# A transformer layer on one core: the last query tile's products are spread over the first attention step, and the first score maxima move one tile earlier

## The reference

```
x = x + attention(layernorm(x))
x = x + ffn(layernorm(x))

attention(h):   q = h @ Wq              # 32 heads of 32 features
                k, v = h @ Wkv          # one key head and one value head, shared by all
                scores = q k^T / sqrt(32) + slope[head] * (key position - query position)
                scores = -inf above the diagonal
                return (softmax(scores) @ v) @ Wo
ffn(h):         w = (6-bit codes of qweight - zero_point) * scale
                return h @ w^T + bias
```

## Time and profile before

| | us |
|---|---|
| median of 3 runs | 813.38 |
| lowest and highest | 812.87, 813.59 |
| the profiled execution's own time | 815.24 |
| its span | 813.5 |
| PE busy | 802.1 (99% of the span) |
| DVE busy | 596.2 (73%) |
| ACT busy | 370.5 (46%) |
| POOL busy | 427.7 (53%) |

### The profile page before, as it was taken

One profiled execution on the slowest core, in us unless ns is written; L12 is line 12 of the kernel. 1 busy time (PEld: TensorE's weight loads), 2 busy tenths in 40 slices (PEclk: granted clock), 3 DMA queues, 4 the chain that ended last, 5 costly groups with the idle time before them and its releaser, 6 DMA issues.

```text
span 813.5 us, 13624 instructions
## 1 busy us (share of the span) xinstructions
PE 802.1 (99%) x4608; PEld 582.3 (72%) x4608; DVE 596.2 (73%) x1592; ACT 370.5 (46%) x728; POOL 427.7 (53%) x311
## 2 busy tenths in 40 slices
PE   7999999999999999999999999999999999999997
PEld 5788888888656555656565555688887888888886
DVE  5885575657878889988888997364647779684878
ACT  2757355312466777676666665221401141041322
POOL 1000000000389988899898888522746288363465
PEclk9999999999999999999999999999999999999999
DMA  9867666566556555665556645452064523500112
GB/s 344 309 216 250 226 242 231 174 191 195 159 133 147 134 144 144 153 160 134 133 159 168 166 108 178 153 176 90 1 226 146 171 79 111 191 35 1 39 66 104
DMA packets 71389, 125.84 MB, mean 155 GB/s; under 512 B 7460, under 2 KB 16708, under 8 KB 71240
## 3 DMA queue, kind: packets, MB, share of 16 engines
q1 hardware_dynamic: 70592, 123.66, 49.6%
q10 hardware_dynamic: 728, 1.32, 0.5%
HBM read 85.61 MB, written 38.94 MB: 153 GB/s over the span
## 4 chain that ended last, share of the span: by engine, by line
PE 91%; DMA 4%; POOL 2%; DVE 1%; issue 1%; ACT 1%; ACTq 0%; SPq 0%; DVEq 0%; POOLq 0%
PE p_s L869 12%; PE p_st L898 10%; PE p_o L909 10%; PE p_o L808 7%; PE p_s L808 6%; PE p_o L922 5%; PE p_s L977 5%; PE p_s L979 5%; PE p_s L978 5%; PE p_o L810 4%; PE p_s L810 3%; PE p_s L1001 3%; PE p_s L1002 3%; PE p_st L1002 2%; PE p_st L1001 2%; PE p_st L977 2%
## 5 line engine op out<-in xcount | busy, mean ns | idle before, releaser
L1462 DVE CUSTOM_DVE_ANT_0 spill<-p_s,mask 128x128 bf16<-128x128 f32 (+3 forms) x512 | 219.5, 483 | 41.2 <-PE p_s L869 40.9
L1168 ACT ACTIVATE pt<-p_st 128x512 f32<-128x512 f32 (+1 forms) x352 | 178.1, 562 | 101.8 <-PE p_st L898 101.6
L637 POOL TENSOR_SCALAR_AFFINE_SELECT pt<-pt 128x512 f32<-128x512 f32 x128 | 88.0, 700 | 234.7 <-ACT pt L1168 234.7
L869 PE MATMUL p_s<-kst,xt 98*128 98x128 f32 (+3 forms) x512 | 151.3, 343 | 0.9 <-DVE mx L1462 0.7
L898 PE MATMUL p_st<-xt,kst 100*128 100x512 f32 (+1 forms) x352 | 129.7, 388 | 0.3 <-ACT pt L1168 0.2
L869 PEld LDWEIGHTS p_s<-kst,xt 98*128 98x128 f32 x512 | 91.7, 189 | 52.9 <-DVE mx L1462 42.5
L644 POOL TENSOR_TENSOR pt<-pt 128x1536 f32<-128x1536 f32 x32 | 112.3, 3508 | 2.7
L909 PE MATMUL p_o<-pt,vst 128*32 128x512 f32 (+3 forms) x1024 | 83.1, 442 | 0.0
L650 POOL TENSOR_TENSOR pt<-pt 128x1024 f32<-128x1024 f32 x32 | 76.7, 2396 | 0.0
L898 PEld LDWEIGHTS p_st<-xt,kst 100*128 100x128 f32 x352 | 64.7, 191 | 13.6 <-issue 5.6
L808 PE MATMUL p_o<-xt,wqh 128*128 128x512 f32 x136 | 53.1, 400 | 0.8 <-DVE xt L1618 0.8
(11 more groups left out here) (206 smaller groups left out, 1619.4 us busy)
## 6 DMA issues: line engine op xcount, KB each, us to landing
xt<-qh_d SPq DMA_DIRECT2D x64, 256.0 KB
qh_d<-qh SPq DMA_DIRECT2D x32, 256.0 KB, 2.1
ql_d<-ql SPq DMA_DIRECT2D x32, 256.0 KB, 2.2
xt<-ql_d SPq DMA_DIRECT2D x32, 256.0 KB
o_d<-o_st SPq DMA_DIRECT2D x32, 256.0 KB, 2.1
ob<-o_d SPq DMA_DIRECT2D x32, 256.0 KB, 4.6
xs<-in_x_t_dram SPq DMA_DIRECT2D x28, 256.0 KB, 5.4
xin<-in_x_dram SPq DMA_DIRECT2D x14, 512.0 KB, 5.9
```

What stands on the lines that cost most here:

```text
L637: pool.affine_select(out=own, in_=own, compare_op=ALU.is_ge, fill=0.0, base=0, pattern=[[0, 4], [1, P]], channel_multiplier=-1).then_inc(c ...
L869: pe.matmul(scores_of(n), qst[s % 4][0:R_MAX, j, qb * P:(qb + 1) * P], kst[0:R_MAX, b * S:b * S + keys], start=True, stop=True).then_inc(s ...
L1168: act.activation(pt[s % 2][:, j:j + heads, PT_AT[kb]:PT_AT[kb] + KB_LEN[kb]], p_st[:, place(k) % 3, 0:heads * KB_LEN[kb]].rearrange("p (j ...
L1462: dve.tensor_tensor_reduce(spill[:, SPILL_AT[qb]:SPILL_AT[qb] + keys], scores_of(n), mask[:, S - keys:S], 1.0, LOWEST, ALU.add, ALU.max, m ...
```

## The change

The 24 products of the last batch's last q tile (tile 7; tile 31 counted over all batches) leave the projection and are dealt out over attention step 0: in front of each of the first four scores or units (x or u) stand two of them, in front of each of the next sixteen stands one. The first 32 scores and their maxima, with the two transposes behind them, move one q tile up: the first four stand in tile 2 in place of tile 3, and so on. The scaling of tile 31 on DVE moves behind maximum 46 (the 15th of step 0), its low part into step 1; ACT takes its high part in step 1; SP stores it in step 1. The exponentials of step 0 go to a buffer of their own, `pt_first`, which lies over `xs` and `xin` (x is no longer needed there), so that they need not wait for the last product; those of step 1 now wait for it. `cut`, `add`, `values` and `totals` take the buffer from `pt_of(s)` (these three parts of the diff are left out below).

DVE, in the last batch's projection from `q_low` of tile 1 on; first before, then after. The `ISA` rows are the maxima (each with the reading of its result behind it).

```diff
--- before
+++ after
@@ -137,6 +137,11 @@
             sb("place_of_q", [P, 2 * CK, S])
             pt = [sb(f"pt{i}", [P, 4, PT_ROW]) for i in range(2)]
             o_st = sb("o_st", [P, S])
+
+        with ExitStack() as stage:
+            sb = tensors(stage)
+            sb("up_to_x", [P, 6 * CK + 5, S])
+            pt_first = sb("pt_first", [P, 4, PT_ROW])
 
 
         sb = tensors(ctx, "right")
@@ -249,7 +254,7 @@
 
         UNPACK = {2: 0, 6: 1}
 
-        EARLY = {3: (4, 0, 4), 4: (0, 4, 8), 5: (0, 12, 8), 6: (0, 20, 8), 7: (0, 28, 4)}
+        EARLY = {2: (4, 0, 4), 3: (0, 4, 8), 4: (0, 12, 8), 5: (0, 20, 8), 6: (0, 28, 4)}
 
         TURN_IN = ((5, 3), (4, 0), (4, 0))
         x_rows = x.rearrange("b s d -> (b s) d")
@@ -273,6 +278,9 @@
 
         BANK, BANK_AT = (0, 0, 1, 2), (0, P, 0, 0)
         BANK_LAST = (1, 1, 2, 3)
+
+        def pt_of(s):
+            return pt_first if s == 0 else pt[s % 2]
 
         def xt(b, low):
             return (xt0 if b % 2 == 0 else xt1)[:, CK * low:CK * low + CK, :]
@@ -398,6 +406,13 @@
                     at_least(sp, unpacked, e)
                     sp.wait_ge(sq_done, BY_ACT.index(7) + 1)
                     sp.dma_start(qw[:, :], qw_v[e // 4, max(e % 4 - 1, 0)]).then_inc(qw_in, 16)
+
+            def store_q(b, m):
+                n = CK * b + m
+                sp.wait_ge(qh_done, n + 1)
+                sp.dma_start(qh_d[b, m], qh[:, m % 2, :].bitcast(F32)).then_inc(q_out[m % 2], 16)
+                sp.wait_ge(ql_done, n + 1)
+                sp.dma_start(ql_d[b, m], ql[:, m % 2, :].bitcast(F32)).then_inc(q_out[m % 2], 16)
 
             def project(b):
                 more = b < LASTB
@@ -411,16 +426,12 @@
                     load_codes(2 * b)
                     sp.wait_ge(q_done, CK * LASTB)
                     load_q(0)
-                for m in range(CK):
-                    if not more and m in (6, 7):
-                        store_max(m - 6)
+                for m in range(CK if more else CK - 1):
+                    if not more and m in (5, 6):
+                        store_max(m - 5)
                     if not more and m in (2, 4, 6):
                         load_q(m // 2)
-                    n = CK * b + m
-                    sp.wait_ge(qh_done, n + 1)
-                    sp.dma_start(qh_d[b, m], qh[:, m % 2, :].bitcast(F32)).then_inc(q_out[m % 2], 16)
-                    sp.wait_ge(ql_done, n + 1)
-                    sp.dma_start(ql_d[b, m], ql[:, m % 2, :].bitcast(F32)).then_inc(q_out[m % 2], 16)
+                    store_q(b, m)
                     if more and m == TURN_M[b] - 1:
                         store_stats(b + 1)
                     if more and m == TURN_M[b]:
@@ -471,7 +482,7 @@
                 if 0 < s < STEPS - 1:
                     store_max(s + 1)
                 if s == 1:
-                    sp.wait_ge(ql_done, CK * B)
+                    store_q(LASTB, CK - 1)
                     for i in range(2):
                         sp.wait_ge(q_out[i], 32 * (B * CK // 2))
                     sp.wait_ge(wt_out, 16 * 2 * B)
...
@@ -837,15 +848,16 @@
                         queries(b, m, c, 2)
                     if b == 0 and c == 5:
                         turn_stats(0)
-                for m in range(together, CK):
+
+                for m in range(together, CK if b < LASTB else CK - 1):
                     for c in range(CK):
                         for what in range(3):
                             queries(b, m, c, what)
                         if b == LASTB and m in EARLY and 0 <= c - EARLY[m][0] < EARLY[m][2]:
                             score(EARLY[m][1] + c - EARLY[m][0])
-                        if b == LASTB and (m, c) == (6, 0):
+                        if b == LASTB and (m, c) == (5, 0):
                             turn_max(0)
-                        if b == LASTB and (m, c) == (7, 5):
+                        if b == LASTB and (m, c) == (6, 5):
                             turn_max(1)
                         if b < LASTB and (m, c) == TURN_IN[b]:
                             turn_stats(b + 1)
...
@@ -935,7 +947,12 @@
 
             def attend(s):
                 n, units, groups = 4 * (4 * s + AHEAD), 0, 0
+
+                q_left = [(c, what) for c in range(CK) for what in range(3)] if s == 0 else []
                 for what in ORDER:
+                    for _ in range(2 if len(q_left) > 16 else 1):
+                        if q_left and what in "ux":
+                            queries(LASTB, CK - 1, *q_left.pop(0))
                     if what == "u":
                         score_t(s, units)
                         units += 1
@@ -1110,27 +1127,27 @@
                 at_least(act, kt_done, 4 * b)
                 act.copy(kv[:, :], p_kv[64:P, :]).then_inc(kv_low, 1)
 
+            def q_high(n):
+                m = n % CK
+                act.wait_ge(q_freed, n + 1)
+                at_least(act, q_out[m % 2], 32 * (n // 2))
+                act.copy(qh[:, m % 2, :], qt[:, m % 2, :]).then_inc(qh_done, 1)
+
             def project(b):
                 more = b < LASTB
                 if 0 < b < LASTB:
                     for t in range(TPB):
                         statistics(4 * b + 4 + t)
-                for m in range(CK):
+                for m in range(CK if more else CK - 1):
                     n = CK * b + m
-                    if not more and m in (6, 7):
-                        max_high(m - 6)
+                    if not more and m in (5, 6):
+                        max_high(m - 5)
                     if not more and m == 5:
                         act.activation(mv[:, 0, 3:4], eps[:, 0:1], ACT.Exp).then_inc(table_in, 1)
-
-                    if n == CK * B - 1:
-                        exponentials(0, 0)
-                        exponentials(0, 1)
                     if more and m == CK - 1:
                         for c in CENTRE[m]:
                             x_high(b + 1, c)
-                    act.wait_ge(q_freed, n + 1)
-                    at_least(act, q_out[m % 2], 32 * (4 * b + m // 2))
-                    act.copy(qh[:, m % 2, :], qt[:, m % 2, :]).then_inc(qh_done, 1)
+                    q_high(n)
                     if m == (2 if b == 0 else 0):
                         low_weights(b)
                     if b == 0 and m == 0:
@@ -1164,8 +1181,11 @@
                 if k == 0:
                     at_least(act, pv_done, s - 1)
                     if s == 0:
+                        act.wait_ge(x_lo, CK * B)
+                        act.wait_ge(sq_done, TILES - TPB)
+                    if s == 1:
                         act.wait_ge(q_done, CK * B)
-                act.activation(pt[s % 2][:, j:j + heads, PT_AT[kb]:PT_AT[kb] + KB_LEN[kb]],
+                act.activation(pt_of(s)[:, j:j + heads, PT_AT[kb]:PT_AT[kb] + KB_LEN[kb]],
                                p_st[:, place(k) % 3, 0:heads * KB_LEN[kb]].rearrange("p (j q) -> p j q", j=heads),
                                ACT.Exp).then_inc(exp_done, 1)
 
@@ -1189,8 +1209,9 @@
                 for k in range(NU):
                     if k == TURN_AT and 0 < s < STEPS - 1:
                         max_high(s + 1)
-                    if (s, k) not in ((0, 0), (0, 1)):
-                        exponentials(s, k)
+                    exponentials(s, k)
+                    if (s, k) == (1, 1):
+                        q_high(CK * B - 1)
                     if k == 0 and s % GROUPS == 1 and s > GROUPS:
                         take_sums(s // GROUPS - 1)
                     if k == 8 and s > 0:
@@ -1407,14 +1428,14 @@
 
             def project(b):
                 more = b < LASTB
-                for m in range(CK):
+                for m in range(CK if more else CK - 1):
                     n = CK * b + m
                     if not more and m in EARLY:
                         for i in range(EARLY[m][2]):
                             maximum(EARLY[m][1] + i)
-                            if m == 6 and i == 2:
+                            if m == 5 and i == 2:
                                 max_low(0)
-                    if not more and m == 7:
+                    if not more and m == 6:
                         max_low(1)
 
                     if more and m == CK - 1:
@@ -1434,8 +1455,7 @@
                         unpack(2 * b + UNPACK[m])
                     elif ahead:
                         centre(b + 1, CENTRE[m][0])
-                    if n < CK * B - 1:
-                        q_low(n)
+                    q_low(n)
                     if 0 < b < LASTB and m in (0, 1):
                         for t in (2 * m, 2 * m + 1):
                             rstd(4 * b + 4 + t)
@@ -1483,7 +1503,9 @@
                 for i in range(16):
                     if first + i < 4 * HEADS_ALL:
                         maximum(first + i)
-                    if s == 0 and i == 11:
+                    if s == 0 and i == 14:
+                        scaled_q(CK * B - 1)
```

(9 more changed lines are left out.)

## The result

| | before | after |
|---|---|---|
| median, us | 813.38 | 817.47 |
| runs | 7 (812.87 to 813.59) | 7 (815.53 to 818.58, and one of 3732.99) |
| profiled execution, us | 815.24 | 815.53 |
| its span and clock | 813.5, 0.997 | 813.8, 0.999 |

The ratio after to before is 1.0041, with a 95% interval of 1.0031 to 1.0052; the execution of 3732.99 us is left out of it, and so is one of 879.84 us of the kernel before in what follows. The change is slower by 0.4%, more than the 0.2% that a measurement can tell. The forecast was 814.3 and "within 0.2%"; the time is also outside the range of 811.9 to 815.6.

A forecast was written before the change was run, and what follows sets the result against it. PE, busy 99%, was taken as the bound, losing about 3.8 us to waits for DVE and a slow clock. -3.3 + 2.6 + 0.2 + 1.4 = +0.9 on the 813.38 median gave 814.3, range 811.9 to 815.6.

The forecast's parts named there:

- The wait in tile 3: Last projection: PE waits 2.6 us at the fifth score for maxima held behind the keys, then 0.2 at the ninth.
- Rival 2: Tile 3: PE's wait is absent or small, so the gain stays, 810.1 us; chance 0.09.
- the gain of 3.3 us in and behind step 0: From tile 31's first product to score s52: 16.7 us before, 13.4 after with PE never idle.
- the old fall of the clock: Beginning of step 1 before the change: 3.41 us at 0.51 clock, about 1.7 us lost, expected to go.
- The scaling of tile 31 between maxima: End of step 0: DVE's scaling delays the bank that score s51 needs, charged in full at 0.6 us.
- the new fall: Tile 3, at the new wait: the clock falls once, costing 1.4 us; forecast of wait and one fall, chance 0.60.
- Rival 3: From about 185 us: the clock stays low for two stretches, +2.6 us, 816.0; chance 0.11.
- ACT, POOL and SP cost nothing: Steps 0 and 1: ACT and POOL have no more to do, SP's stores cost nothing, at most 0.5 us.

The follow-up runs named there:

- moved_alone: Kernel before with only the first 32 scores, their maxima and transposes one q tile up, tile 31's products kept together; 818.08 us, ratio 1.0046.
- control: The kernel before, measured once more with no edit; 814.34 us, ratio 1.0001.
- half_tile_sooner: Changed kernel with the first 32 scores half a tile later and DVE scaling tile 31 one maximum sooner; 813.26 us, ratio 0.9985.
- after_low_later: Changed kernel with DVE taking tile 31's low part two maxima later in step 1; 816.71 us, ratio 1.0033.
- again: The changed kernel, measured once more with no edit; 816.52 us, ratio 1.0029.
- room_2: Kernel before with ten unread matmuls dealt out ahead of the first ten scores and units of step 0; 821.22 us, ratio 1.0088.

## Why the prediction was wrong, point by point

**The wait in tile 3: right.** 2.6 and 0.2 were forecast, 2.62 and 0.19 measured, and moved_alone shows them alone. Rival 2, that the wait would not be there, is out.

**The step that failed: the gain of 3.3 us in and behind step 0, of which 1.4 us was the old fall of the clock.** The prediction credited s48 to s52 with 3.94 - 2.36 = 1.6, "nearly all of it the clock". The profiled execution of before held that fall; the median, to which the sum was added, did not. Without a fall these four scores take 2.54, in control and in moved_alone, so that there was 0.2 to win.

The sentence that led there was "Both kernels share what lies around the span". Around the span lie 815.24 - 813.5 = 1.7 us in before and 815.53 - 813.8 = 1.7 in after, so that part was right. But I took the profiled execution's 1.9 us above the median to be of that kind. It lay inside the span, and it was mainly the fall, 1.4. The range of 812.87 to 813.59 over the runs, with the profile at 815.24, could have told me: the profiled execution was unlike them.

**What else was mis-sized in the 3.3.** By moved_alone against the changed kernel, both without a fall, the products dealt out gain 2.11 up to s48, where the prediction's terms give 2.3 (12.78 before and 10.4 after). The step's part of the gain was thus right. The scaling of tile 31 between maxima was charged at 0.6; s48 to s52 loses 0.67, of which half_tile_sooner got 0.43 back by the scaling's place alone, and the wait before s51 is 0.53. That s52 to s68 loses 0.36 was not priced at all. Together 2.11 - 0.67 - 0.36 = 1.1, and the position of s68 says 1.05.

**Luck in the base.** The row 205.62 is not tile 31's first product but its fourth. s28 stands behind the tile's first block, and that block begins at 204.86:

```profile
204.86 0.40 PE L808 MATMUL p_o<-xt,wqh 128*128 128x512 f32 x1
...
205.56 0.22 PE L869 MATMUL p_s<-kst,xt 98*128 98x128 f32 x1
```

So "the same work" was not the same. From 205.62 to s32 stand 21 products, three scores and a transpose, set against 24 products alone. They take 211.16 - 205.62 = 5.54, and 24 products 5.44, so the three products left out and the three scores and the transpose taken in cancel to 0.1 us. A smaller slip is in the forecast's own range: gains of 3.0 to 3.9, waits of 2.8 and a clock of 0.9 to 1.7 give 813.2 to 814.9, not 813.4 to 815.1. Neither changes the outcome.

**The clock: right in kind, wrong in form.** I gave the new fall 0.60 as if an execution either always has it or never. By the count at 0.998 every kernel with the wait has it in a part of its executions: 9 of 16 for the change, 4 of 6 in after_low_later, 2 of 5 in moved_alone; none of 17 where PE was given work. At 0.997 or less these are 8, 2 and none. It costs 1.29 (forecast 1.4). By the rule of the Trainium skill that the prediction cited (page "TensorE: Matmul & The Clock Gate", section "Why this matters for your kernels") one gap of this length leaves the clock up; again's profile, with a fall 1 us behind a gap of 2.46, and the 10 to 15 falls in these 27 executions speak against it as the only rule, as the earlier trace rows did. Rival 3, a fall over two stretches, was seen in room_2 at a wait of 3.71 us (6.8 us low), not in a profile of the changed kernel.

**ACT, POOL and SP cost nothing: wrong for POOL.** "ACT and POOL do not have more to do" is true and was not the question. Tile 31's low part had moved on DVE to a place where POOL's add runs. It lasts 1.60 there, and s52 to s68 takes 0.36 longer.

**The sum.** The scores moved up cost 2.89 (moved_alone: the waits of 2.8 and 0.1 more), and the products dealt out gain 1.05: +1.84 without any fall, which is where s68 lies (60.68 - 58.84). With a fall of 1.3 in about half of the executions the median comes to between 1.8 and 3.1 above before. Measured were 2.5 in again and, in the first measurement with a fall in four of its six ordinary executions, 3.3 by the ratio (interval 2.5 to 4.2). Without any fall the medians differ by 1.6 or 2.2, by which executions are taken, so that 1.84 lies between. They can't be told closer: from s68 to the end of the span the profiles take 581.7 to 582.7 us whatever the kernel, and before and control, which are the same program, 581.8 and 582.6. What makes that difference stays open.

**Not settled:** what in the old step 0 sets off before's fall in 6 to 12 of 89 executions. That it needs the lull there was argued, not shown.

## What to carry to other kernels

Before a gain is worked out from one profiled execution, put its time beside the runs: if it lies above all of them, find out what it holds that they don't, above all a stretch at the lower clock, and take that out of the base. Before a stretch is called the same work in two kernels, count its instructions in both. Work that is moved earlier on PE moves the demand for whatever it waits on; here a chain on another engine (the keys) had not moved, and half a tile less had the gain at no wait. When an instruction moves on DVE, look at what POOL runs at its new place, not only at what stands before and behind it in its own queue.

## What the runs showed of the hardware

- A fall of the clock is a matter of chance in one and the same program: it came in 6 to 12 of 89 executions of before, in 10 to 15 of 27 of kernels with the wait in front of s4 (2.46 us in all four profiles of them), and in all 5 of the kernel whose profile has a wait of 3.71 us.
- With the idle stretch before s4 at 1.33 us in place of 2.46 no fall came in 7 executions, and with it at 0.20 none in 10.
- A DVE subtraction with two SBUF inputs, 0.69 us by itself, took 3.88, 1.60, 1.48 and 1.04 us where POOL's adds and selects ran. In the last three cases it ended 0.54 to 0.55 us behind the end of POOL's select, though the add in front of that had ended before. It is not always so: in half_tile_sooner it took 1.45, ended 0.55 behind the add, and the select behind it took 1.10 in place of 0.64.

```profile
221.67 1.45 DVE L1427 TENSOR_TENSOR ql<-qt,qh 128x512 fp32r<-128x512 f32 x1
```

```profile
220.17 2.40 POOL L663 TENSOR_TENSOR pt_first<-pt_first 128x1024 f32<-128x1024 f32 x1
222.52 1.10 POOL L650 TENSOR_SCALAR_AFFINE_SELECT pt<-pt 128x512 f32<-128x512 f32 x1
```
